# Decoder of two layers: the order of steps in the context product, and of the first expert block's preparation in layer 1

## The chip, the cores and the metric

The kernel runs on one core of one Trainium2 chip. The metric is the device time of one execution in microseconds (us), as the median of the runs shown. A core has five engines, each with its own queue that it works through in program order: PE (TensorE, matrix products), DVE (VectorE), ACT (ScalarE), POOL (GpSimd) and SP (SyncE, which here only issues DMA transfers). The engines wait for one another through semaphores, and an instruction that waits holds up everything behind it on its engine.

## What is computed

A decoder of two layers over x of 4 batches x 512 tokens x 256 features. Cut to what the change touches:

```python
x = x + attn0(layernorm(x))                       # causal, 16 heads
# context product, the same context for all three factors
x1 = einsum('eth,efh->etf', layernorm(x), ctx)    # 512 x 256 by 512 x 256, for each of 4 batches
x2 = x1
x = x + einsum('etf,efh->eth', gelu(x1) * x2, ctx)
x = x + moe0(layernorm(x))                        # 8 experts of width 512, two per token, and a shared one
x = x + attn1(layernorm(x)); x = x + cross(layernorm(x), ctx)
# layer 1's experts: 8 of width 1024, the best two per token, weighted
for e in range(8):
    h = silu(x @ w1[e].T) * (x @ w3[e].T)
    out = out + wte[:, e:e+1] * (h @ w2[e].T)
x = x + out
```

## The kernel before

The stages stand one behind the other, each in a block of its own: attention, `geglu` (the context product), `moe` for layer 0, two attentions, `moe` for layer 1.

**The context product** (`geglu`, L948) goes batch by batch. Its parts are written once for each engine, and `run` gives all engines the same order of steps: LN (normalise a batch: DVE statistics, two small POOL operations, four DVE operations that write `xn`), T (eight PE transposes into `t_ps`, two DVE copies to `xnT`), G (eight PE products into the four banks of `g_ps`; for each bank ACT forms `gelu`, then DVE multiplies it into `h`), Y (two halves of eight PE products into `y_ps`, each added to x by DVE), IN (SP loads the context). The profile lists each product of G and Y twice, so that G has sixteen rows there and each Y sixteen. Batch 0's LN and T come first. Then a hardware loop runs over batches 0 to 2 with the body in `body(b, nxt)`, and the same body without a next batch follows for batch 3. In the body, LN and T of the next batch stand between steps of this one.

**The experts of layer 1** (`moe`, with `moe_schedule` as the order that all engines share). Tokens are sorted into blocks of rows, each with one expert: blocks 0, 1 and 2 are large (256 rows), block 3 is small, and so on. A block n is worked in chunks f = 0 to 3 of the hidden width. All float32 weights and rows are split in two parts, hi (ACT copies) and lo (DVE subtracts), and a product is made in three passes. The steps and what they stand for:

- SPOT and LIST: which token stands in which row (one-hot products on PE). LISTS and GATHER: the lists are read and POOL gathers the first rows.
- UNMASKED, EXP, SHARES: the routing weights (DVE, ACT for the exponential, DVE). WEIGHTS: POOL multiplies them into `held`, six operations. LIST with part 2: 64 PE products that bring the weights into row order, which read `held` and the one-hot tiles. These tiles lie in the memory of `raw2`, so that block 0's w2 is loaded (WEIGHED, on SP) only when they have been read; WEIGHED on DVE reads the result.
- T n: rows of block n transposed on PE, split by ACT and DVE (`rows_hi`, `rows_lo`); POOL gathers the rows of block n + 2.
- C 0 f: split of w1 and w3 of block 0, chunk f (ACT two operations, DVE two); SP then loads the same chunk for block 1. W n f: the same for block n, and the load for n + 1.
- CV: split of block 0's w2 (four operations on ACT, four on DVE); SP then loads block 1's. V n f: the same for later blocks.
- G n f: 24 PE products into one of two slots of `g_ps`; ACT forms silu, DVE multiplies (`late`, the step's `h_made`). The slot is free for the chunk after next once DVE has done so. H n f: the split of that product (`h_hi` on ACT, `h_lo` on DVE).
- Y n t: 24 PE products with w2 for half t of block n. Y 0 0 waits for the whole of CV, and for WEIGHED.
- IDLE: products without use that keep PE at work.

`chunk(n, f)` writes G, then the W that `weights_beside(n, f)` names, then H (in the last chunk of a block H comes ahead of W), then what `between` has at the number n * 4 + f. For block 0 the W beside chunk f is W 1 f, and CV stands in `between` at chunk 1.

Semaphores carry all of this. A step changes place on all engines at once, since one list sets the order for all.

Of the kernel before, what the change touches and what calls it, by code (L numbers as in the profile page):

```python
# [29 lines left out]
B, T, D = 4, 512, 256  # L30
# [914 lines left out]
def geglu(nc, tag, x, const, w):  # L945


    with ExitStack() as ctx:  # L948
# [40 lines left out]
        def run(eng, do):  # L989
            def step(kind, *at):  # L990
                if kind in do:
                    do[kind](*at)

            step("LN", 0)
            step("T", 0)

            def body(b, nxt):
                step("IN", b)
                step("G", b)
                if nxt is not None:  # L1000
# [180 lines left out]
def moe_schedule(shared, nf):  # L1181
# [4 lines left out]
    def small(n):  # L1186
        return n >= nshared and halves(n - nshared) == 1
# [32 lines left out]
    else:  # L1220
# [24 lines left out]
        yield "C", 0, 0  # L1245
        yield "UNMASKED", 1, 0
        yield "EXP", 1, 0
        yield "C", 0, 1

        yield "IDLE", 24, 0  # L1250
        yield "T", 0, 0
        yield "IDLE", 5, 0
        yield "SHARES", 0, 0
        yield "WEIGHTS", 0, 0
        for f in range(2, nf):
            yield "C", 0, f
        between = {1: [("LIST", c, 2) for c in range(NSPOT)] + [("WEIGHED", 0, 0), ("CV", 0, 0)]}

    def prepared(n, *chunks):
        if n < nblocks:  # L1260
            for f in chunks:
                yield "W", n, f


    def weights_beside(n, f):
        if nf > 2 and n and small(n - 1):
            return (n + 1, f - 1) if f else (n, nf - 1)
        if nf > 2 and n > 1 and small(n - 2) and f == 0:
# [990 lines left out]
```

## Time and profile before

| | us |
|---|---|
| median of 3 runs | 1727.65 (1726.07 to 1731.89) |
| time of the profiled execution | 1731.58 |
| span of its profile | 1729.8 |
| PE busy | 1489.5 (86%) |
| DVE busy | 1177.9 (68%) |
| ACT busy | 900.3 (52%) |
| POOL busy | 553.0 (32%) |
| context product, from the first IDLE product to the last product | 300.3 to 376.3 |
| layer 1's experts, last PE product of the first token list to the first product of Y 0 0 | 1339.5 to 1380.8 |

Times in the profile count from the span's start. PE, DVE, ACT and POOL are busy times; the stages have different limits, so that the shares say little and the order of time in a stage says much. "Idle before" in a row is the time for which the engine stood still ahead of it, and the name behind the arrow is what ended that.

### The profile page before, as it was taken

How to read it: one execution, taken by the hardware profiler on the slowest of the kernel's cores; microseconds unless marked ns; L12 is line 12 of the kernel's file. 1: busy time of each engine (PE TensorE's matmuls, PEld its weight loads, DVE VectorE, ACT ScalarE, POOL GpSimd, SP SyncE). 2: the span in 40 equal slices, each digit the busy share in tenths (PEclk: the TensorE clock that was granted, in tenths of full speed). 3: DMA queues.
4: the chain of work that ended last, by engine and by line, in shares of the span. 5: the costliest groups of instructions: out<-in, count | busy, mean ns of one | idle time of the engine just before them, and what ended most of it. 6: DMA issues, size and time to landing. Idle time of an engine off the chain costs nothing. (4 is left out here: it accounts for less than half of the span.)

```text
span 1729.8 us, 30585 instructions
## 1 busy us (share of the span) xinstructions
PE 1489.5 (86%) x10462; PEld 1015.4 (59%) x10462; DVE 1177.9 (68%) x2008; ACT 900.3 (52%) x1704; POOL 553.0 (32%) x765
## 2 busy tenths in 40 slices
PE   7989987889899996798888878878864799999996
PEld 3445453559899996333333333223223699999996
DVE  5565552454778885667677636776767778888884
ACT  2444453123256664146555465676761466767763
POOL 6344440010236554725343340110011323333321
PEclk8999998998999999789999989888887899999999
DMA  6223220220258884422222131222203468777782
GB/s 166 43 44 57 43 52 7 65 88 32 98 178 248 249 255 114 129 57 52 41 43 63 35 68 39 62 50 52 45 14 133 163 205 244 241 237 239 247 232 65
DMA packets 104266, 194.36 MB, mean 112 GB/s; under 512 B 30417, under 2 KB 55762, under 8 KB 101170
## 3 DMA queue, kind: packets, MB, share of 16 engines
q1 hardware_dynamic: 75186, 157.78, 29.3%
q0 software_dynamic: 28416, 34.25, 11.2%
q8 instruction: 84, 1.38, 0.3%
q14 instruction: 68, 0.56, 0.1%
q10 hardware_dynamic: 512, 0.40, 0.1%
HBM read 135.63 MB, written 18.61 MB: 89 GB/s over the span
## 5 line engine op out<-in xcount | busy, mean ns | idle before, releaser
L719 ACT ACTIVATE l1a_sb_probs<-l1a_s_ps,l1a_sb_kmax 128x512 f32<-128x512 f32 x256 | 172.5, 708 | 74.2 <-issue 59.8
L617 DVE TENSOR_REDUCE l1a_sb_mx<-l1a_s_ps 128x2 f32<-128x1024 f32 x128 | 154.2, 1219 | 62.7 <-PE l1a_s_ps L805 62.7
L651 DVE TENSOR_REDUCE l1a_sb_kmax<-l1a_s_ps 128x2 f32<-128x1024 f32 x128 | 154.1, 1216 | 45.2 <-PE l1a_s_ps L846 44.2
L725 ACT ACTIVATE l1a_sb_probs<-l1a_s_ps 128x1024 f32<-128x1024 f32 x128 | 128.0, 1022 | 89.4 <-PE l1a_s_ps L846 88.8
L617 DVE TENSOR_REDUCE l0a_sb_mx<-l0a_s_ps 128x2 f32<-128x256 f32 (+3 forms) x128 | 103.5, 821 | 77.4 <-PE l0a_s_ps L818 76.0
L1927 PE MATMUL l1m_g_ps<-l1m_sb_rows_hi,l1m_sb_hi 128*128 128x256 f32 x512 | 147.2, 287 | 6.8 <-DVE l1m_sb_late L1825 6.4
L846 PE MATMUL l1a_s_ps<-l1a_sb_qst,l1a_sb_kst 49*128 49x512 f32 (+1 forms) x512 | 130.4, 516 | 24.1 <-ACT l1a_sb_probs L719 22.5
L846 PEld LDWEIGHTS l1a_s_ps<-l1a_sb_qst,l1a_sb_kst 49*128 49x128 f32 (+1 forms) x512 | 50.1, 195 | 168.8 <-issue 86.5
L1927 PE MATMUL l1m_g_ps<-l1m_sb_rows_lo,l1m_sb_hi 128*128 128x256 f32 x512 | 145.7, 285 | 0.0
L1927 PE MATMUL l1m_g_ps<-l1m_sb_rows_hi,l1m_sb_lo 128*128 128x256 f32 x512 | 145.7, 284 | 0.0
L1799 DVE TENSOR_TENSOR l1m_sb_lo<-l1m_sb_raw,l1m_sb_hi 128x512 fp32r<-128x512 f32 x184 | 121.8, 704 | 19.6 <-ACT l1m_sb_hi L1710 18.7
L1660 POOL DMA_INDIRECT out_x<-l1m_sb_late,l1m_sb_add_to x39 | 65.7, 1684 | 176.0 <-DVE l1m_sb_late L1847 171.1
L725 ACT ACTIVATE l0a_sb_probs<-l0a_s_ps 128x1024 f32<-128x1024 f32 (+3 forms) x128 | 87.3, 698 | 64.3 <-PE l0a_s_ps L818 64.1
L1927 PE MATMUL l0m_g_ps<-l0m_sb_rows_hi,l0m_sb_hi 128*128 128x256 f32 x384 | 113.7, 296 | 7.1 <-DVE l0m_sb_rows_lo L1793 6.6
L507 POOL DMA_DIRECT2D l1a_sb_kst<-l1a_sb_hi x156 | 76.8, 496 | 133.1 <-PE l1a_s_ps L846 128.9
L1927 PE MATMUL l0m_g_ps<-l0m_sb_rows_hi,l0m_sb_lo 128*128 128x256 f32 x384 | 111.7, 291 | 0.0
L1927 PE MATMUL l0m_g_ps<-l0m_sb_rows_lo,l0m_sb_hi 128*128 128x256 f32 x384 | 111.6, 291 | 0.0
L1710 ACT ACTIVATE l1m_sb_hi<-l1m_sb_raw 128x512 fp32r<-128x512 f32 x184 | 104.8, 620 | 0.0
L1927 PEld LDWEIGHTS l1m_g_ps<-l1m_sb_rows_hi,l1m_sb_hi 128*128 128x128 f32 x512 | 99.2, 194 | 7.4 <-issue 6.6
L1927 PEld LDWEIGHTS l1m_g_ps<-l1m_sb_rows_hi,l1m_sb_lo 128*128 128x128 f32 x512 | 99.1, 194 | 0.0
L1927 PEld LDWEIGHTS l1m_g_ps<-l1m_sb_rows_lo,l1m_sb_hi 128*128 128x128 f32 x512 | 99.0, 193 | 0.0
L507 POOL DMA_DIRECT2D l0a_sb_kst<-l0a_sb_hi x124 | 61.2, 498 | 98.5 <-PE l0a_s_ps L818 59.4
(410 smaller groups left out, 4018.3 us busy)
## 6 DMA issues: line engine op xcount, KB each, us to landing
l1m_sb_raw<-in_l1m_w SPq DMA_DIRECT2D x92, 512.0 KB
l0m_sb_raw<-in_l0m_w SPq DMA_DIRECT2D x72, 512.0 KB
l1m_sb_raw<-in_l1m_w SPq DMA_DIRECT2D x23, 1024.0 KB
l1a_sb_qst<-l1a_sb_hi SPq DMA_DIRECT2D x256, 32.0 KB, 2.0
l1a_sb_kst<-l1a_sb_hi POOLq DMA_DIRECT2D x156, 32.0 KB, 2.0
l0a_sb_qst<-l0a_sb_hi SPq DMA_DIRECT2D x128, 32.0 KB, 2.0
l1a_sb_qst<-l1a_sb_lo SPq DMA_DIRECT2D x128, 32.0 KB, 2.0
l0a_sb_kst<-l0a_sb_hi POOLq DMA_DIRECT2D x124, 32.0 KB, 2.0
```

What stands on the lines that cost most here:

```text
L507: pool.dma_start(in_stack(kst, p, e, n), in_part(source, i, p, e)).then_inc(kstacked[p], 16)
L617: dve.tensor_reduce(mx[:, g, qt, 2 * p:2 * p + 2], buffer("A", b, g, j)[:, :, 0:last], AX.X, ALU.max).then_inc(a_max.sem, 1)
L651: dve.tensor_reduce(kmax[:, n % 4, :], buffer("S", b, g, j)[:, :, :], AX.X, ALU.max, negate=True).then_inc(kmax_done.sem, 1)
L719: ins = act.activation(probs[:, n % 8, e, :], at[:, e, :], ACT.Exp, bias=kmax[:, n % 4, e:e + 1], accum_out=zsum[:, n % 4, e:e + 1])
L725: act.activation(probs[:, n % 8, :, c0:T], at[:, :, c0:T], ACT.Exp, scale=SCALE).then_inc(exp_done.sem, 1)
L846: ins = pe.matmul(at[:, e, c0:T], kst[rows, p, kt * P:(kt + 1) * P], qst[rows, p, c0:T], start=True, stop=not causal)
L1660: pool.indirect_dma_start(total, bass.IndirectOffsetOnAxis(ap=at, axis=0), y[:, e % 2, t, :], None, compute_op=ALU.add).then_inc(stored[e ...
L1710: ins = act.activation(two_chunks(hi, s % 2, f), raw13[:, s % n13, f, n, :, :], ACT.Copy)
L1799: ins = dve.tensor_tensor(two_chunks(lo, s % 2, f), raw13[:, s % n13, f, n, :, :], two_chunks(hi, s % 2, f).bitcast(F32), ALU.subtract)
L1927: ins = pe.matmul(at, s, m, start=n == 0, stop=n == len(passes) - 1)
```

## The change

In the context product's body, LN of the next batch moves ahead of this batch's G, and T of the next batch moves from between the two Y to ahead of both. In `moe_schedule`, for the layer whose blocks have four chunks (layer 1): SHARES and WEIGHTS move from behind T 0 to ahead of the idle products and T 0; C 0 1 moves from ahead of the idle products to behind T 0; C 0 2 and C 0 3 move from ahead of G 0 0 to behind G 0 0 and G 0 1; the W of block 1 move one chunk back, with W 1 3 directly ahead of G 1 0; CV moves from behind chunk 1 of block 0 to behind chunk 0 of block 1. Layer 0's experts keep their order.

```diff
             def body(b, nxt):
                 step("IN", b)
+
+                if nxt is not None:
+                    step("LN", nxt)
                 step("G", b)
                 if nxt is not None:
-                    step("LN", nxt)
+                    step("T", nxt)
                 step("Y", b, 0)
-                if nxt is not None:
-                    step("T", nxt)
                 step("Y", b, 1)
...
         yield "UNMASKED", 1, 0
         yield "EXP", 1, 0
-        yield "C", 0, 1
+        yield "SHARES", 0, 0
+        yield "WEIGHTS", 0, 0
 
         yield "IDLE", 24, 0
         yield "T", 0, 0
         yield "IDLE", 5, 0
-        yield "SHARES", 0, 0
-        yield "WEIGHTS", 0, 0
-        for f in range(2, nf):
-            yield "C", 0, f
-        between = {1: [("LIST", c, 2) for c in range(NSPOT)] + [("WEIGHED", 0, 0), ("CV", 0, 0)]}
+        yield "C", 0, 1
+
+        between = {1: [("LIST", c, 2) for c in range(NSPOT)] + [("WEIGHED", 0, 0)], nf: [("CV", 0, 0)]}
...
     def weights_beside(n, f):
-        if nf > 2 and n and small(n - 1):
+        if nf > 2 and n == 0:
+
+            return (1, f - 1) if f else (1,)
+        if nf > 2 and small(n - 1):
             return (n + 1, f - 1) if f else (n, nf - 1)
...
+        if nf > 2 and n == 1 and f == 0:
+            yield from prepared(1, nf - 1)
         yield "G", n, f
+        if nf > 2 and n == 0 and f < 2:
+            yield "C", 0, f + 2
```

In the context product's loop, PE's queue from the last bank of G to the loop's end, before: `l0g_y_ps` is Y, `l0g_t_ps` the transposes T; the rows without names are register work.

```order
L1085 MATMUL l0g_g_ps<-l0g_sb_xnT,l0g_sb_ctxT 128x512 x2
L58 ISA x2
L1096 MATMUL l0g_y_ps<-l0g_sb_ctxN,l0g_sb_h 128x256 x8
L58 ISA
L58 REGISTER_ALU
L1075 MATMUL l0g_t_ps<-const_ident,l0g_sb_xn 128x128 x8
L58 REGISTER_ALU
L1096 MATMUL l0g_y_ps<-l0g_sb_ctxN,l0g_sb_h 128x256 x8
```

And after:

```order
L1086 MATMUL l0g_g_ps<-l0g_sb_xnT,l0g_sb_ctxT 128x512 x2
L58 ISA
L58 REGISTER_ALU
L1076 MATMUL l0g_t_ps<-const_ident,l0g_sb_xn 128x128 x8
L58 ISA x2
L1097 MATMUL l0g_y_ps<-l0g_sb_ctxN,l0g_sb_h 128x256 x8
L58 REGISTER_ALU
L1097 MATMUL l0g_y_ps<-l0g_sb_ctxN,l0g_sb_h 128x256 x8
```

The transposes now stand directly behind G, and the two Y are back to back.

DVE's queue in the same loop, before, from the end of LN (`l0g_sb_xn`) to the end of the body: add of Y's first half to x, the two copies of T, add of the second half. The four products of the gates (`l0g_sb_h`) and LN's statistics stand ahead of this.

```order
L1132 TENSOR_SCALAR l0g_sb_xn<-x_sb,l0g_sb_mv,l0g_sb_rstd 128x256 x4
L58 REGISTER_ALU
L1040 ISA
L1040 TENSOR_TENSOR x_sb<-l0g_y_ps,x_sb 128x512
L58 REGISTER_ALU
L1047 COPY l0g_sb_xnT<-l0g_t_ps 128x512 x2
L1040 ISA
L1040 TENSOR_TENSOR x_sb<-l0g_y_ps,x_sb 128x512
```

And after:

```order
L1133 TENSOR_SCALAR l0g_sb_xn<-x_sb,l0g_sb_mv,l0g_sb_rstd 128x256 x4
L58 ISA
L1036 TENSOR_TENSOR l0g_sb_h<-l0g_g_ps,l0g_sb_gelu 128x512 x4
L58 REGISTER_ALU
L1048 COPY l0g_sb_xnT<-l0g_t_ps 128x512 x2
L58 REGISTER_ALU
L1041 ISA
L1041 TENSOR_TENSOR x_sb<-l0g_y_ps,x_sb 128x512
L1041 ISA
L1041 TENSOR_TENSOR x_sb<-l0g_y_ps,x_sb 128x512
```

The four gate products now stand behind the whole of LN, and the copies stand directly behind them.

DVE's queue in layer 1's experts, before, from WEIGHED (`row_holds`, `row_weight`) on. L1805 is CV, L1825 the gate product of a chunk, L1799 the lo part of a w1 and w3 chunk (two each), L1831 the lo part of the gate product.

```order
L2149 COPY l1m_sb_row_holds<-l1m_y_ps 128x2x69
L2151 TENSOR_TENSOR l1m_sb_row_weight<-l1m_sb_row_holds 128x46
L2152 TENSOR_TENSOR l1m_sb_row_weight<-l1m_sb_row_weight,l1m_sb_row_holds 128x46
L1805 TENSOR_TENSOR l1m_sb_lo<-l1m_sb_raw,l1m_sb_hi 128x512 x4
L1825 TENSOR_TENSOR l1m_sb_late<-l1m_g_ps,l1m_sb_late 128x512
L1799 TENSOR_TENSOR l1m_sb_lo<-l1m_sb_raw,l1m_sb_hi 128x2x256 x2
L1831 TENSOR_TENSOR l1m_sb_h_lo<-l1m_sb_late,l1m_sb_h_hi 128x512
```

And after, the stretch of the same queue that ends with CV (now L1812), from the gate product of chunk 3 of block 0 on; in this version the gate product is L1832, the w1 and w3 parts L1806, the lo part of the gate product L1838:

```order
L1832 TENSOR_TENSOR l1m_sb_late<-l1m_g_ps,l1m_sb_late 128x512
L1838 TENSOR_TENSOR l1m_sb_h_lo<-l1m_sb_late,l1m_sb_h_hi 128x512
L1806 TENSOR_TENSOR l1m_sb_lo<-l1m_sb_raw,l1m_sb_hi 128x2x256 x4
L1832 TENSOR_TENSOR l1m_sb_late<-l1m_g_ps,l1m_sb_late 128x512
L1806 TENSOR_TENSOR l1m_sb_lo<-l1m_sb_raw,l1m_sb_hi 128x2x256 x2
L1838 TENSOR_TENSOR l1m_sb_h_lo<-l1m_sb_late,l1m_sb_h_hi 128x512
L1812 TENSOR_TENSOR l1m_sb_lo<-l1m_sb_raw,l1m_sb_hi 128x512 x4
```

CV stood directly behind WEIGHED, ahead of the gates of chunks 2 and 3 of block 0; it now stands behind these two, behind W 1 1 to W 1 3 and W 2 0, and behind the gate of chunk 0 of block 1.

## Rows read from the trace of the kernel before

**Rows 1.** The page, part 1: PE's busy time, share of the span and instructions.
```profile
PE 1489.5 (86%) x10462; PEld 1015.4 (59%) x10462; DVE 1177.9 (68%) x2008; ACT 900.3 (52%) x1704; POOL 553.0 (32%) x765
```

**Rows 2.** Timeline, PE, context product (start us, length us, instructions, idle before).
```profile
325.08 7.03 PE L1085 MATMUL l0g_g_ps<-l0g_sb_xnT,l0g_sb_ctxT 128*128 128x512 f32 x16
333.68 3.71 PE L1096 MATMUL l0g_y_ps<-l0g_sb_ctxN,l0g_sb_h 128*128 128x256 f32 x16 [1.57 <-DVE l0g_sb_h L1035]
338.49 1.09 PE L1075 MATMUL l0g_t_ps<-const_ident,l0g_sb_xn 128*128 128x128 f32 x8 [1.10 <-DVE l0g_sb_xn L1132]
339.42 3.62 PE L1096 MATMUL l0g_y_ps<-l0g_sb_ctxN,l0g_sb_h 128*128 128x256 f32 x16
342.87 7.03 PE L1085 MATMUL l0g_g_ps<-l0g_sb_xnT,l0g_sb_ctxT 128*128 128x512 f32 x16
```

**Rows 3.** Timeline, DVE, context product.
```profile
305.76 1.29 DVE L1047 COPY l0g_sb_xnT<-l0g_t_ps 128x512 f32<-128x512 f32 x2 [0.75 <-PE l0g_t_ps L1075]
...
325.41 0.69 DVE L1040 TENSOR_TENSOR x_sb<-l0g_y_ps,x_sb 128x512 f32 x1 [2.74 <-PE l0g_y_ps L1096]
329.09 1.29 DVE L1035 TENSOR_TENSOR l0g_sb_h<-l0g_g_ps,l0g_sb_gelu 128x512 f32<-128x512 f32 x2 [2.99 <-ACT l0g_sb_gelu L1061]
...
332.85 0.69 DVE L1035 TENSOR_TENSOR l0g_sb_h<-l0g_g_ps,l0g_sb_gelu 128x512 f32<-128x512 f32 x1 [1.02 <-ACT l0g_sb_gelu L1061]
333.46 1.40 DVE L1119 BATCH_NORM_STATS2 l0g_sb_stats<-x_sb 128x6 f32 x4
...
336.98 1.38 DVE L1132 TENSOR_SCALAR l0g_sb_xn<-x_sb,l0g_sb_mv,l0g_sb_rstd 128x256 f32 x4 [1.51 <-POOL l0g_sb_rstd L1111]
```

**Rows 4.** Timeline, PE, layer 1's experts, blocks 0 and 1.
```profile
1359.98 2.02 PE L1899 MATMUL l1m_y_ps<-l1m_sb_held,l1m_sb_raw 128*128 128x69 bf16 x32 [3.48 <-issue]
1361.82 1.62 PE L1899 MATMUL l1m_y_ps<-l1m_sb_held,l1m_sb_late 128*128 128x69 bf16 x32
...
1375.70 0.55 PE L1927 MATMUL l1m_g_ps<-l1m_sb_rows_hi,l1m_sb_hi 128*128 128x256 f32 x1 [6.44 <-DVE l1m_sb_late L1825]
...
1379.68 0.36 PE L1927 MATMUL l1m_g_ps<-l1m_sb_rows_hi,l1m_sb_hi 128*128 128x256 f32 x1
...
1380.83 0.36 PE L1927 MATMUL l1m_y_ps<-l1m_sb_hi,l1m_sb_h_hi 128*128 128x256 f32 x1
...
1383.78 0.28 PE L1927 MATMUL l1m_g_ps<-l1m_sb_rows_hi,l1m_sb_hi 128*128 128x256 f32 x1
```

**Rows 5.** Timeline, ACT, layer 1's experts.
```profile
1346.13 0.31 ACT L1693 ACTIVATE l1m_sb_l<-l1m_sb_l 128x128 f32<-128x128 f32 x1 [4.31 <-DVEq L2042]
...
1371.72 2.19 ACT L1717 ACTIVATE l1m_sb_hi<-l1m_sb_raw 128x512 fp32r<-128x512 f32 x4 [8.82 <-DMA l1m_sb_raw<-in_l1m_w]
```

**Rows 6.** Timeline, SP, the issue of the first two loads of w2.
```profile
1364.72 11.30 SPq L1531 DMA_DIRECT2D l1m_sb_raw<-in_l1m_w  x2
```

**Rows 7.** Timeline, POOL, the six products of WEIGHTS.
```profile
1353.04 6.85 POOL L1677 TENSOR_TENSOR l1m_sb_held<-l1m_sb_own,l1m_sb_share 128x368 bf16<-128x368 bf16 x6 [1.92 <-DVEq L2090]
```

**Rows 8.** Timeline, DVE, layer 1's experts.
```profile
1349.31 0.69 DVE L1793 TENSOR_TENSOR l1m_sb_rows_lo<-l1m_t_ps,l1m_sb_rows_hi 128x512 fp32r<-128x512 f32 x1 [0.51 <-issue]
...
1353.04 4.97 DVE L1799 TENSOR_TENSOR l1m_sb_lo<-l1m_sb_raw,l1m_sb_hi 128x512 fp32r<-128x512 f32 x4
1357.94 0.68 DVE L1825 TENSOR_TENSOR l1m_sb_late<-l1m_g_ps,l1m_sb_late 128x512 f32<-128x512 f32 x1
...
1372.45 2.50 DVE L1805 TENSOR_TENSOR l1m_sb_lo<-l1m_sb_raw,l1m_sb_hi 128x512 fp32r<-128x512 f32 x4 [7.61 <-ACT l1m_sb_hi L1717]
...
1375.47 1.28 DVE L1799 TENSOR_TENSOR l1m_sb_lo<-l1m_sb_raw,l1m_sb_hi 128x512 fp32r<-128x512 f32 x2
...
1387.49 0.69 DVE L1825 TENSOR_TENSOR l1m_sb_late<-l1m_g_ps,l1m_sb_late 128x512 f32<-128x512 f32 x1 [2.66 <-ACT l1m_sb_late L1736]
```

**Rows 9.** Windows: busy of PE, PEld, DVE, ACT, POOL (instructions), granted clock, DMA share, GB/s.
```profile
1375.00:1380.00 5.00, 4.30 (x21) 4.33 (x22) 3.96 (x7) 3.21 (x6) 0.00 (x0) 0.52 0.58 211
```

**Rows 10.** Waits of PE from 1380 us to the end (total, times, longest).
```profile
PE l1m_y_ps L1927 <- issue: 3.2, 2, 2.8
```

## The prediction

> **What bounds the kernel now.** I read the page first: PE is busy for 1489.5 us of 1729.8, the largest share [rows 1], so what counts is where PE stands still or works slowly, and who ends that. Then PE's timeline in the two stages that the change touches, and beside each of its gaps the timeline of the engine named there.
>
> *Context product.* One turn of the loop takes 342.87 - 325.08 = 17.79 us of PE [rows 2]. In it the reader is to see two gaps: 1.57 us ahead of the first Y, until DVE has multiplied the last gate, and 1.10 us ahead of the transposes T, until DVE has normalised the next batch. From the first Y to the next G it is 342.87 - 333.68 = 9.19 us. DVE starts LN only when the last gate is done (at 333.46), and LN runs to 336.98 + 1.38 = 338.36, 4.90 us [rows 3].
>
> *Layer 1's experts.* PE waits twice between the first rows and Y 0 0 [rows 4]. 3.48 us, until 1359.98, ahead of the products that order the weights: POOL works on WEIGHTS until 1353.04 + 6.85 = 1359.89 [rows 7]. And 6.44 us, until 1375.70, ahead of G 1 0: it needs the slot of G 0 2, whose gate stands on ACT and DVE behind CV; ACT stood 8.82 us in front of CV for w2's transfer, until 1371.72 [rows 5]. Behind that wait PE is also slow: 19 products from 1375.70 to 1379.68, 0.21 us each, and the granted clock in this window is 0.52, the lower level of 1.2 GHz; from 1379.68 on it is 0.12 us (24 products from 1380.83 to 1383.78) [rows 4, 9]. After 1380 PE waits for 3.2 us in all up to the end [rows 10]: PE bounds the rest, and what is won before Y 0 0 reaches the end of the kernel.
>
> **The context product after the change.** T moves into the gap ahead of the first Y. T keeps PE for 339.42 - 338.49 = 0.93 us, the gap is 1.57 us, and xn must be there by then. The two Y then stand back to back at 342.87 - 339.42 = 3.45 us each, 6.90 together; the old 9.19 us shrink by 2.29 us in each of the three turns, 6.9 us in all.
>
> What it costs is that the gates now queue behind LN on DVE. In a turn that begins with G at time 0, DVE ends the last add at 325.41 + 0.69 - 325.08 = 1.02 us [rows 2, 3]; LN then takes 4.90 us (its 1.51 us wait for POOL included) and ends at 5.92. T needs it at 7.03, when G ends: free by 1.1 us. The gates started at 4.01 before; now the first three of them run from 5.92, 0.61 us each (333.46 - 332.85), to 7.75, and the fourth waits for its gelu until 7.77 (332.85 - 325.08) as before. So LN is hidden in the time in which DVE waited for gelu, with nothing to spare: whatever DVE takes to go round the loop moves the first Y one to one, in two turns (the first turn has 1 us to spare: there LN starts when the copies of batch 0 end, 305.76 + 1.29 = 307.05 [rows 3], and with them G). No row shows that time alone. Its bounds: nothing (PE goes round without a gap, 339.42 + 3.45 = 342.87), and 2.99 us, the idle time in which it lies before [rows 3]. I take 0.2 us, near PE's, since DVE too only steps a counter and branches: 0.4 us for two turns. The copies of T follow the fourth gate, and DVE has nothing else before the adds; POOL's two operations keep their distance to LN; SP's step IN keeps its place. Gain 6.9 - 0.4 = **6.5 us**, with bounds 6.9 and 6.9 - 2 x 2.95 = 1.0.
>
> **Layer 1's experts after the change.** I walk through the queues.
>
> *SHARES first.* The exponential ends at 1346.44 [rows 5]. SHARES fills the time from the end of rows_lo, 1350.00, to 1353.04: 3.0 us [rows 8]. Now it runs from 1346.5 to 1349.5, where DVE waited and did C 0 1; T 0's rows_lo follows at 1349.5 instead of 1349.31, and G 0 0 starts 0.2 us later. POOL starts WEIGHTS at 1349.7 and, if it is as slow as before (6.85 us), ends at 1356.5. PE ends G 0 1 at 1359.98 - 3.48 + 0.2 = 1356.7: the first wait is gone. C 0 1 to C 0 3 are hidden: POOL's products make a DVE lo part cost 4.97 / 4 = 1.24 us instead of 1.28 / 2 = 0.64 [rows 8], so C 0 1 is done at 1350.2 + 2.5 = 1352.7, before G 0 1 wants it at 1353.6; C 0 2 and C 0 3 at 1357.7 and 1360.2 at the latest, before 1359.6 and 1362.5.
>
> Beside POOL's products, the DVE row with a source in PSUM keeps its 0.68 us (1357.94) [rows 8], so I charge rows_lo nothing. The Trainium skill ("SBUF — State Buffer", section "SBUF: two separate sides") has DVE with two inputs in SBUF contend with GpSimd for a port pair held as an exclusive lock; rows_lo has one input there and escapes by it as well. Were it slowed like the others, G 0 0 would start 0.6 us later and the gain be 0.6 us less.
>
> *To the end of G 0 3.* The weights' products take 2 x 1.45 = 2.9 us at their second half's pace to 3.3 us as before (1363.27 - 1359.98, where the first 32 took 1.84) [rows 4], so G 0 2 starts at 1359.6 to 1360.0. G 0 2 and G 0 3 take 2.95 us each: G 0 3 ends at 1365.5 to 1365.9. G 1 0 has its slot (gate of G 0 2 at about 1364.4) and W 1 0, runs at once and ends at 1368.4 to 1368.8, T 2 0.5 us later.
>
> *Then a new wait.* Y 0 0 needs CV, and CV now stands last in a long queue on DVE. From the gate of G 0 3 on DVE has the list that the order shows: gate, h_lo, four lo parts, gate, two lo parts, h_lo, CV's four: 14 operations, 13 x 0.61 + 0.68 = 8.6 us, and 1.1 us of handovers from ACT (0.7 ahead of the h_lo, 0.35 ahead of W 1 2), 9.7 us. The gate comes 0.8 us behind its chunk's end on PE (1387.49 against 1383.78 + 2.9) [rows 4, 8]. Y 0 0 can start at 1365.7 + 0.8 + 9.7 = 1376.2, after a wait of about 7 us. Before it started at 1380.83: 4.6 us earlier. W2's load is hidden: SP issues it behind the load for W 1 0 at about 1362.7, 2.0 us earlier than before (1364.72 [rows 6]); before it took 7.0 us to 1371.72, so it lands at 1369.7, and ACT wants it at 1372.1. The price of this cover, should it fail, is one to one.
>
> *And the clock.* The new wait is as long as the old one of 6.44 us, behind which 19 products ran at the lower level. The same 19 products of Y 0 0 would lose 3.98 - 19 x 0.12 = 1.7 us. The next chunk, G 1 1, starts 4.6 - 1.7 = **2.9 us** earlier than at 1383.78. Bounds: 4.6 (no slow products) and 1.0 (each of DVE's six lo parts of w1 and w3 stretched by 0.3 us). From the skill's page "TensorE: Matmul & The Clock Gate", section "What's actually happening": the same kernel shows 6, 11 or 14 slow products depending on the phase. By 6 instead of 19 the loss would be 0.6 us and this gain 4.0; the trace here has 19, and I stay with them.
>
> Behind CV, w2 of block 1 is asked for at about 1377.3 instead of 1376.0; V 1 0 waits for Y 0 1, not before 1386.5, and 7 us lie between: free.
>
> **The sum.** 6.5 + 2.9 = 9.4 us. The profiled execution took 1731.58 us, 3.9 above the median; it would become 1722.2, and the median 1727.65 - 9.4 = **1718.2 us**.
>
> **The rivals.**
> - *CV's wait costs all of it.* DVE's chain to CV ends 4.6 - 1.7 = 2.9 us or more later than I have it (POOL's gathers beside the lo parts, or w2 landing after 1375), and only the context product gains: 1727.65 - 6.5 = 1721.2. For it: the chain is long and I have each operation at its best pace. Against: POOL's products are over by 1356.5, and behind them two lo parts take 1.28 us [rows 8].
> - *Both waits go and none comes.* Then the experts win 3.48 + 6.44 + 1.7 = 11.6 us: 1709.5. Against: the order puts CV behind the 14 operations, and nothing else holds Y 0 0.
> - *DVE's way round the loop is dear.* With 1.6 us in place of 0.2 the context product gains 6.9 - 3.1 = 3.8 us: 1727.65 - 3.8 - 2.9 = 1721.0.
> - *Slower.* w2 is late at CV. It is issued behind two loads of 0.5 MB for block 1 and 2. Each microsecond that it lands after 1372.1 moves Y 0 0. To eat both gains and 0.3% more it would have to land 6.5 + 2.9 + 5.2 = 14.6 us late, at 1386.7, 24 us after its issue against 7.0 before: 1732.8 or more.
> - *The change doesn't do what it says.* The order shows every move on every engine; no weight on this.
>
> **Chances.** Mine 0.66; CV costs all 0.14; loop dear 0.09; both waits gone 0.07; slower 0.02; nothing won, by an effect that I don't see, 0.02. My own case spans 1714.7 (bounds 6.9 and 4.6, and 1.5 us of scatter) to 1721. The range 1712.5 to 1723.0 takes in the two cases at 1721, and leaves out the case at 1709.5 and the worst. A measurement of this kernel tells about 0.3% (5.2 us) from no change; faster by that is below 1722.5: 0.88. Within it: 0.09. Slower: 0.03.
>
> **What would show it.** Right: turns of about 15.7 us in the context product, T directly behind G, PE's only gap about 0.6 us ahead of the first Y; no wait ahead of the weights' products; G 1 0 directly behind G 0 3; a wait of about 7 us ahead of Y 0 0, released by DVE's lo part of w2, with slow products behind it. Wrong: a turn above 16.5 us (the loop); Y 0 0 released by a DMA behind ACT (w2); no wait at Y 0 0 (the chain); or PE waiting more after Y 0 0 than 3.2 us.

## The result and the profile after

In rounds taken in turn with the kernel before, the changed kernel takes 1721.11 us against 1732.03 us (medians of 20 runs each): the ratio is 0.9946, with a 95% interval of 0.9932 to 0.9959. That is 9.3 us less (7.1 to 11.8), where 9.4 were forecast. The two medians by themselves differ by 10.9 us, inside that interval. One of the 12 runs of e1 below took 1796 us at a granted clock of 0.81 and is left out of its ratio. In these rounds the kernel before stood 4.4 us higher than in the three runs that the prediction started from; so the time comes out at 1721.1 where 1718.2 was named.

The profiled execution of the changed kernel took 1731.05 us, the slowest of its 20. Its span, 1729.2 us, stands beside 1729.8 for the kernel before: the two traces seem to show no gain at all. So I read the gain stage by stage, from places that both kernels have in common. The first is the row of idle products ahead of a stage (TensorE, line 98). First the kernel before, then the changed kernel (timeline of PE: start us, length us, instructions, idle before):

```profile
300.30 4.88 PE L98 MATMUL l0g_g_ps<-const_ones_b 128*128 128x512 bf16 x12 [2.32 <-PEq L225]
...
377.36 2.96 PE L98 MATMUL l0m_g_ps<-const_ones_b 128*128 128x512 bf16 x13 [1.05 <-PEq L948]
...
1339.28 5.96 PE L98 MATMUL l1m_g_ps<-const_ones_b 128*128 128x512 bf16 x20
```

```profile
304.69 1.87 PE L98 MATMUL l0g_g_ps<-const_ones_b 128*128 128x512 bf16 x4 [2.32 <-PEq L225]
...
375.18 4.48 PE L98 MATMUL l0m_g_ps<-const_ones_b 128*128 128x512 bf16 x20 [1.05 <-PEq L948]
...
1341.26 4.01 PE L98 MATMUL l1m_g_ps<-const_ones_b 128*128 128x512 bf16 x9
```

| stretch | before | changed | difference |
|---|---|---|---|
| start to the context product | 300.30 | 304.69 | +4.39 |
| context product | 377.36 - 300.30 = 77.06 | 375.18 - 304.69 = 70.49 | **-6.57** |
| to the first idle product of layer 1's experts | 961.92 | 966.08 | +4.16 |
| from there to G 1 1 | 1383.78 - 1339.28 = 44.50 | 1381.69 - 1341.26 = 40.43 | **-4.07** |

In this pair of traces 10.6 us are won in the two places of the change and 8.6 us are lost in two stretches that it doesn't touch. In those TensorE does the same work for longer, at a lower granted clock. In the windows (columns as in [rows 9]) the instructions before the context product are the same to one; first before, then changed:

```profile
0.00:300.50 300.50, 260.13 (x2465) 141.06 (x2466) 159.52 (x270) 125.67 (x201) 118.72 (x221) 0.95 0.27 59
377.50:1339.30 961.80, 799.84 (x4896) 482.76 (x4895) 678.26 (x1145) 514.81 (x1026) 311.95 (x452) 0.91 0.36 95
```

```profile
0.00:304.50 304.50, 264.31 (x2464) 143.73 (x2464) 159.33 (x269) 125.86 (x201) 118.31 (x221) 0.93 0.27 58
375.00:1341.00 966.00, 804.41 (x4889) 484.96 (x4890) 678.60 (x1144) 515.17 (x1026) 313.50 (x452) 0.90 0.36 95
```

2464 matrix products keep PE for 4.2 us more at a clock of 0.93 instead of 0.95. The experiments below show the same stretch between 297.5 and 304.7 us long, whatever the kernel: it belongs to the execution, not to the change. Behind G 1 1 another 1.5 us are lost, all at the kernel's end. There PE stands still for 2.85 us in both kernels. Its last 48 products (the last block's Y) then take 5.71 us from the first start to the last in the kernel before and 7.19 us in the changed one, where 17 of them are 0.21 us apart (granted clock 0.50 from 1711.60 to 1715.00). DVE's last product waits for them, 7.61 us instead of 6.12, and POOL's last writes of the output wait for DVE. This isn't the change's doing either: e3 and e4 below, with the experts' order of before, show 7.20 and 7.19 us. From the first idle product of the experts to the end the pair of traces so shows 390.50 - 387.95 = 2.55 us of the 4.07. PE's waits behind Y 0 0 are 3.2 us in all, as before [rows 10].

**The context product after** (timeline of PE, then of DVE; they answer to [rows 2] and [rows 3]):

```profile
327.27 7.03 PE L1086 MATMUL l0g_g_ps<-l0g_sb_xnT,l0g_sb_ctxT 128*128 128x512 f32 x16
334.14 1.04 PE L1076 MATMUL l0g_t_ps<-const_ident,l0g_sb_xn 128*128 128x128 f32 x8
335.87 7.17 PE L1097 MATMUL l0g_y_ps<-l0g_sb_ctxN,l0g_sb_h 128*128 128x256 f32 x32 [0.70 <-DVE l0g_sb_h L1036]
342.88 1.45 PE L1086 MATMUL l0g_g_ps<-l0g_sb_xnT,l0g_sb_ctxT 128*128 128x512 f32 x3
```

```profile
327.60 0.69 DVE L1041 TENSOR_TENSOR x_sb<-l0g_y_ps,x_sb 128x512 f32 x1 [2.76 <-PE l0g_y_ps L1097]
328.28 1.41 DVE L1120 BATCH_NORM_STATS2 l0g_sb_stats<-x_sb 128x6 f32 x4
...
331.83 1.38 DVE L1133 TENSOR_SCALAR l0g_sb_xn<-x_sb,l0g_sb_mv,l0g_sb_rstd 128x256 f32 x4 [1.50 <-POOL l0g_sb_rstd L1112]
333.12 2.61 DVE L1036 TENSOR_TENSOR l0g_sb_h<-l0g_g_ps,l0g_sb_gelu 128x512 f32<-128x512 f32 x4
335.66 1.28 DVE L1048 COPY l0g_sb_xnT<-l0g_t_ps 128x512 f32<-128x512 f32 x2
```

A turn is 342.88 - 327.27 = 15.61 us. T stands directly behind G, both Y follow in one row of 32, and PE's only gap is 0.70 us ahead of them. On DVE the end of the last add (328.29) and LN's first row (328.28) touch, though the step round the loop lies between them.

**Layer 1's experts after** (timeline of PE; the rows of [rows 4]). To compare with the kernel before, take 1.98 us off, by which the first idle product is later here:

```profile
1358.73 1.21 PE L1906 MATMUL l1m_y_ps<-l1m_sb_held,l1m_sb_raw 128*128 128x69 bf16 x32
1359.78 1.20 PE L1906 MATMUL l1m_y_ps<-l1m_sb_held,l1m_sb_late 128*128 128x69 bf16 x32
1360.81 0.36 PE L1934 MATMUL l1m_g_ps<-l1m_sb_rows_hi,l1m_sb_hi 128*128 128x256 f32 x1
...
1369.53 0.60 PE L1927 MATMUL l1m_t_ps<-const_ident,l1m_sb_rows 128*128 128x128 f32 x4
...
1377.31 0.58 PE L1934 MATMUL l1m_y_ps<-l1m_sb_hi,l1m_sb_h_hi 128*128 128x256 f32 x1 [7.18 <-DVE l1m_sb_lo L1812]
...
1381.69 0.28 PE L1934 MATMUL l1m_g_ps<-l1m_sb_rows_hi,l1m_sb_hi 128*128 128x256 f32 x1
```

No wait is left ahead of the list's products, and they take 2.08 us (3.29 before). G 1 0 has no wait. A wait of 7.18 us stands ahead of Y 0 0, and DVE's lo part of w2 (CV) ends it. Behind it the first 14 products of Y 0 0 are 0.21 us apart and the rest 0.12: the chunk takes 4.38 us instead of 2.95. The list's products of the kernel before ran for the most part at the lower clock, 0.50 in this window of its trace (columns as in [rows 9]); in the changed kernel the clock was 1.00 throughout:

```profile
1360.00:1361.00 1.00, 1.00 (x19) 1.00 (x19) 1.00 (x3) 1.00 (x3) 0.97 (x1) 0.50 0.83 332
```

The wait's cause in the timelines of DVE and SP (they answer to [rows 8] and [rows 6]):

```profile
1367.48 0.69 DVE L1832 TENSOR_TENSOR l1m_sb_late<-l1m_g_ps,l1m_sb_late 128x512 f32<-128x512 f32 x1
...
1369.91 2.54 DVE L1806 TENSOR_TENSOR l1m_sb_lo<-l1m_sb_raw,l1m_sb_hi 128x512 fp32r<-128x512 f32 x4 [0.35 <-ACT l1m_sb_hi L1717]
...
1374.77 2.48 DVE L1812 TENSOR_TENSOR l1m_sb_lo<-l1m_sb_raw,l1m_sb_hi 128x512 fp32r<-128x512 f32 x4
```

```profile
1364.38 0.33 SPq L1538 DMA_DIRECT2D l1m_sb_raw<-in_l1m_w  x1
```

From the gate of G 0 3 (1367.48) to CV's end (1377.25) it is 9.8 us, without a gap longer than 0.7: DVE's queue is the wait. ACT's part of CV starts at 1373.62 behind other work of ACT, not behind a DMA: the load of w2 is hidden, by 1.5 us (7.7 us from its issue at 1364.38 to its landing). POOL's six products of WEIGHTS take 5.50 us here (6.85 in [rows 7]), since only part of them meets work of DVE. In their time rows_lo keeps its 0.69 us (at 1351.70), and the two lo parts behind it take 1.94 us instead of 1.29. By the Trainium skill ("SBUF — State Buffer", section "SBUF: two separate sides") a DVE operation with two inputs in SBUF contends with a GpSimd operation that reads SBUF for a shared pair of ports; the trace agrees, with 1.94 us for the two lo parts (both inputs in SBUF) and an unchanged 0.69 us for rows_lo (one input in SBUF).

### The profile page after: what moved, and what is told of

The parts are those of the page before. It is cut to its first block and busy times, and to the rows that moved or that the text cites. A ratio compares the mean times of both kernels' runs of the same rounds, so it can differ in the third digit from the quotient of the medians.

```text
span 1729.2 us, 30572 instructions
## 1 busy us (share of the span) xinstructions
PE 1498.6 (87%) x10462; PEld 1021.1 (59%) x10462; DVE 1175.8 (68%) x2008; ACT 900.7 (52%) x1704; POOL 551.7 (32%) x765
## 5 line engine op out<-in xcount | busy, mean ns | idle before, releaser
L1806 DVE TENSOR_TENSOR l1m_sb_lo<-l1m_sb_raw,l1m_sb_hi 128x512 fp32r<-128x512 f32 x184 | 119.3, 691 | 18.4 <-ACT l1m_sb_hi L1717 17.6
L1934 PE MATMUL l1m_y_ps<-l1m_sb_hi,l1m_sb_h_hi 128*128 128x256 f32 x312 | 90.9, 291 | 10.4 <-DVE l1m_sb_lo L1812 7.2
```

Of the source, the lines that this page charges most:

```text
L1806: ins = dve.tensor_tensor(two_chunks(lo, s % 2, f), raw13[:, s % n13, f, n, :, :], two_chunks(hi, s % 2, f).bitcast(F32), ALU.subtract)
L1934: ins = pe.matmul(at, s, m, start=n == 0, stop=n == len(passes) - 1)
```

## The experiments

Where times are compared inside a stage, zero is the first of the 24 idle products ahead of T 0 ("+" below). **G 1 1** is +44.50 us before and +40.43 after the change. A later mark, the first product of the G chunk behind block 1's early ones (1434.46 before, 1432.37 changed), is called **mark B**: +95.18 and +91.11. In the changed kernel the gain is the same at both, 4.07 us. These are single executions. Where the experts' order is that of before, G 1 1 is at +44.50, +44.14 (e1), +44.00 (e3) and +44.54 (e4); where it is the changed one, at +40.43, +40.41 (e2) and +41.14 (a1). So the experts' gain at this mark is 2.9 to 4.1 us, and a shift of half a microsecond in one trace says nothing.

### One half of the change at a time

**e1: the context product alone** (the first piece of the change's diff; the second stage as before).

> Only the context product's part of the change; the experts keep the order of before. My theory: the two parts add, and this one gives 6.5 us (6.6 in the trace of the changed kernel, from the first idle product of the stage to the first of the next: 77.06 us become 70.49), so the time is 0.9962 of before. Rival A: the gain in the stage is given back further on, because the stages behind it start elsewhere in the clock's course; then the stage is 6.6 us shorter and the time is within 2 us of before. Rival B: the clock phase makes the gain, the order does not; then the stage is longer than 72 us here.

Measured: 1724.46 us against 1730.39, ratio 0.9963 (0.9945 to 0.9981), 6.4 us less (3.3 to 9.5): rivals A and B are both out, by the time and by the stage. The stage takes 367.95 - 297.47 = 70.48 us, 6.58 less than before, and the turns are the changed kernel's. In the experts the list's wait of 3.48 us is there, and G 1 0 still waits for the gate:

```profile
1360.57 0.56 PE L1928 MATMUL l1m_g_ps<-l1m_sb_rows_hi,l1m_sb_hi 128*128 128x256 f32 x1 [5.97 <-DVE l1m_sb_late L1826]
```

**e2: the experts alone** (the other pieces of the diff).

> Only the experts' part of the change; the context product keeps the order of before. My theory: 4.1 us (the changed kernel's trace has G 1 1 at 40.43 us behind the first of the 24 idle products, before it was 44.50), 0.9976 of before; a wait of about 7.2 us at Y 0 0, released by DVE's lo part of w2. Rival: I forecast 2.9 us from the same chain with 19 slow products and slow list products; then G 1 1 stands 41.6 us behind the first idle product and the changed kernel was lucky by 1.2.

Measured: 1727.0 against 1730.39, ratio 0.998 (0.9965 to 0.9995), 3.5 us less (0.9 to 6.1). The context product takes 375.59 - 298.55 = 77.04 us, as before. Y 0 0 starts at +36.05, G 1 1 at +40.41, mark B at +91.09: each within 0.02 us of the changed kernel. The rival's +41.6 doesn't show here; a1 below, at +41.14, comes half way to it.

```profile
1373.51 0.58 PE L1933 MATMUL l1m_y_ps<-l1m_sb_hi,l1m_sb_h_hi 128*128 128x256 f32 x1 [7.19 <-DVE l1m_sb_lo L1811]
```

What follows: the halves don't touch each other. Ratios multiply to 0.9943 against 0.9946 for the whole, and the stages add up: 6.58 + 4.09 = 10.7 us against 10.6.

### Inside the context product

**e3: LN ahead of G, T left between the two Y.**

```diff
 step("IN", b)
-step("G", b)
 if nxt is not None:
     step("LN", nxt)
+step("G", b)
 step("Y", b, 0)
 if nxt is not None:
     step("T", nxt)
 step("Y", b, 1)
```

> Of the context product only LN ahead of G; T stays between the two Y. My theory: the wait of 1.10 us ahead of T goes, T itself (0.93 us) stays on PE between the Y, so a turn of the loop is 17.79 - 1.10 = 16.7 us against 15.6 with both, and the stage 3.4 us shorter than before (73.7 us). Rival (LN first is what gives everything, T's place is of no matter): turns of 15.6 us.

**e4: T behind G, LN left behind G's gates.**

```diff
 step("G", b)
 if nxt is not None:
     step("LN", nxt)
+    step("T", nxt)
 step("Y", b, 0)
-if nxt is not None:
-    step("T", nxt)
 step("Y", b, 1)
```

> Of the context product only T ahead of both Y; LN stays behind the gates on DVE. My theory: T waits for LN, which starts when the last gate is multiplied (8.38 us behind G's start) and takes 4.90 us; T then 0.93, two Y 6.90, so a turn is 8.38 + 4.90 + 0.13 + 0.93 + 0.17 + 6.90 = 21.4 us, and the stage 77.1 + 3 x 3.6 = 87.9 us, 10.8 us slower than before. Rival (LN is hidden anyway by the time that PE needs for the gates): turns of 15.6 to 17.8 us. PE idles some 6 us a turn in one gap, so that the lower clock may add 1 us a turn.

Measured, e3: 1723.14 us in one run; the stage 373.46 - 300.36 = 73.10 us, a turn 340.30 - 323.82 = 16.48. PE's timeline has T without a wait and keeps the 1.57 us ahead of the first Y:

```profile
332.42 3.71 PE L1097 MATMUL l0g_y_ps<-l0g_sb_ctxN,l0g_sb_h 128*128 128x256 f32 x16 [1.57 <-DVE l0g_sb_h L1036]
335.97 1.04 PE L1076 MATMUL l0g_t_ps<-const_ident,l0g_sb_xn 128*128 128x128 f32 x8
...
340.30 4.88 PE L1086 MATMUL l0g_g_ps<-l0g_sb_xnT,l0g_sb_ctxT 128*128 128x512 f32 x11
```

Measured, e4: 1750.43 us in one run; the stage 396.95 - 301.54 = 95.41 us, a turn 332.62 - 308.81 = 23.81, 6.0 more than before. The timeline of PE and the windows over T's wait and behind it:

```profile
322.33 1.96 PE L1074 MATMUL l0g_t_ps<-const_ident,l0g_sb_xn 128*128 128x128 f32 x8 [6.39 <-DVE l0g_sb_xn L1131]
324.08 8.70 PE L1095 MATMUL l0g_y_ps<-l0g_sb_ctxN,l0g_sb_h 128*128 128x256 f32 x32
332.62 7.03 PE L1084 MATMUL l0g_g_ps<-l0g_sb_xnT,l0g_sb_ctxT 128*128 128x512 f32 x16
```

```profile
315.70:322.30 6.60, 0.24 (x1) 0.00 (x0) 3.76 (x14) 0.60 (x1) 1.21 (x2) 0.87 0.26 81
322.30:332.60 10.30, 10.27 (x40) 9.02 (x41) 2.08 (x3) 0.00 (x0) 0.00 (x0) 0.75 0.00 0
```

The reader is to see two costs. PE waits 6.39 us for xn, in the place of the old gaps of 1.57 and 1.10: 3.7 us a turn. And T and both Y take 332.62 - 322.33 = 10.29 us, where at the full clock they take 0.93 + 6.90 = 7.8 [rows 2]: 2.4 us more a turn, at a granted clock of 0.75 in that window. I had expected the first cost, and of the second 1 us a turn at most and none in the sum, so 18.3 us were lost and not 10.8.

What follows: LN first wins 3.96 us by itself. T's move by itself loses 18.3, and on top of LN first it wins another 2.6. Only the order LN, G, T, Y, Y has both.

### Inside the experts

**e5: SHARES and WEIGHTS ahead of the idle products, C 0 1 behind T 0 with C 0 2 and C 0 3, all else as before.**

```diff
-yield "C", 0, 1
+yield "SHARES", 0, 0
+yield "WEIGHTS", 0, 0
 yield "IDLE", 24, 0
 yield "T", 0, 0
 yield "IDLE", 5, 0
-yield "SHARES", 0, 0
-yield "WEIGHTS", 0, 0
-for f in range(2, nf):
+for f in range(1, nf):
     yield "C", 0, f
```

> The kernel before with one edit in layer 1's first block: SHARES and WEIGHTS stand ahead of the 24 idle products and of T 0; CV stays between C 0 1 and G 0 0's successors as before, the context product as before. My theory (the two waits are separate, and this edit takes away the first alone): TensorE's idle 3.48 us ahead of the list's second product goes, and the list's products take 2.1 to 3.3 us; the 6.44 us ahead of Y 0 0 are a DMA's (w2 of block 0, which SP issues behind other loads and on which ACT waited 8.82 us), so part of what is won returns there: Y 0 0 starts 1 to 4 us earlier than before's +41.55 us after the first idle product, G 1 0's start likewise. Rival (the waits are one budget: the DMA alone sets Y 0 0): Y 0 0 stays at +41.5 us within 0.3 and the wait ahead of it grows to about 9.9 us.

**e6: CV behind G 0 3 instead of behind the list, all else as before.**

```diff
-between = {1: [("LIST", c, 2) for c in range(NSPOT)] + [("WEIGHED", 0, 0), ("CV", 0, 0)]}
+between = {1: [("LIST", c, 2) for c in range(NSPOT)] + [("WEIGHED", 0, 0)], nf: [("CV", 0, 0)]}
```

> The kernel before with one edit in layer 1's first block: CV (the split of w2 of block 0) stands behind block 0's last gate product instead of ahead of the second gate. My theory: the list's wait of 3.48 us stays; DVE and ACT no longer stand at CV's wait for the DMA while block 0's gates end, and Y 0 0 starts when gate 3's chain and CV's four splits are through: 1.0 us earlier than before's +41.55 us (0.5 to 2.5). Together with the weights-first edit it should make the 5.50 us that Y 0 0 moved in the changed kernel: gains of the two single edits that add to about 5.5 us say they are independent; a sum far below says that each is worth something only with the other. Rival (CV behind the gates costs all its 2.5 us on the path): Y 0 0 at +42 to +44 us.

Measured, e5: the list's wait is gone, and G 1 0 waits for longer (PE). ACT stands in front of the DMA as before, and SP shows why (ACT, then SP):

```profile
1370.73 0.55 PE L1926 MATMUL l1m_g_ps<-l1m_sb_rows_hi,l1m_sb_hi 128*128 128x256 f32 x1 [9.83 <-DVE l1m_sb_late L1824]
```

```profile
1366.75 2.19 ACT L1716 ACTIVATE l1m_sb_hi<-l1m_sb_raw 128x512 fp32r<-128x512 f32 x4 [9.48 <-DMA l1m_sb_raw<-in_l1m_w]
```

```profile
1359.08 11.97 SPq L1530 DMA_DIRECT2D l1m_sb_raw<-in_l1m_w  x2
```

SP issues w2's load at +23.93, behind the loads of w1 and w3 as before and only 1.5 us earlier (+25.44 [rows 6]); w2 is there at 1366.75, +31.60, where it was +32.44 [rows 5]. G 1 0 starts 0.84 us earlier than before, G 1 1 0.45, mark B 0.43. This is the rival's case, close to the letter (Y 0 0 at +41.10, 0.45 earlier where the rival allows 0.3): 3.48 us of wait were taken away and at most 0.45 were won, since the DMA ends the next wait. G 1 1, at +44.06, lies among the four executions with the order of before (+44.00 to +44.54), so even the 0.45 may be nothing.

Measured, e6: Y 0 0 starts at +38.22, 3.3 us earlier than before, where I expected 1.0. But Y 0 0 was the wrong mark: G 1 0 stood behind the wait before, and now stands ahead of it. At G 1 1, behind both, it is +43.50: 1.0 us. At mark B it is 0.64, because the half clock reaches into G 1 1. Nor is the 1.0 us shown to be CV's. The list's products, ahead of CV's new place, take 2.06 us here and 3.29 in the kernel before, and G 0 2 starts 1.07 us earlier. From G 0 2 to G 1 1 it takes 20.59 us here, 20.51 before, and 20.06 to 21.38 in e1, e3 and e4. The list's products differ between executions of one order: in e4, which has the experts' order of before, they run at the full clock too, behind a wait of 2.48 us:

```profile
1376.30 1.19 PE L1898 MATMUL l1m_y_ps<-l1m_sb_held,l1m_sb_raw 128*128 128x69 bf16 x32 [2.48 <-issue]
```

And e6 itself (PE):

```profile
1357.41 1.20 PE L1899 MATMUL l1m_y_ps<-l1m_sb_held,l1m_sb_raw 128*128 128x69 bf16 x32 [2.35 <-issue]
...
1374.78 0.58 PE L1927 MATMUL l1m_y_ps<-l1m_sb_hi,l1m_sb_h_hi 128*128 128x256 f32 x1 [5.99 <-DVE l1m_sb_lo L1805]
```

The list's products still wait for POOL, so that G 0 2 starts at +22.91, where the changed kernel has +19.55, and everything behind it is later.

What follows: at G 1 1, against the four executions with the order of before, e5 alone wins nothing that is clear of their scatter and e6 alone 0.5 to 1.0 us; the whole change wins 2.9 to 4.1. The prediction treated the moves as a walk through one queue and was right to. No run has these two edits together without the change's other moves (C 0 2 and C 0 3 behind the gates, the W of block 1 one chunk back). Leg by leg, as an estimate from the traces: G 0 2 at +19.76 as in e5 and 15.3 us from there to Y 0 0 as in e6 give +35.1, against +36.05 in the changed kernel; w2, which is there at +31.60 in e5, would come about 0.3 us late for ACT. So the two edits may well be enough for the gain, and that the other moves help is not shown.

### What the 7.18 us are

**e7: CV directly behind H 0 3 in the changed kernel; the weight splits of blocks 1 and 2 put off behind it.**

```diff
-between = {1: [...("WEIGHED", 0, 0)], nf: [("CV", 0, 0)]}
+between = {1: [...("WEIGHED", 0, 0)], nf - 1: [("CV", 0, 0)]}
+put_off = {(0, 0): (), (0, 1): (), (0, 2): ((1, 0),), (0, 3): (), (1, 0): ((1, 1), (1, 2)),
+           (1, 1): ((1, 3), (2, 0)), (1, 2): ((2, 1), (2, 2)), (1, 3): ((2, 3),)}
...
-        if nf > 2 and n == 1 and f == 0:
-            yield from prepared(1, nf - 1)
...
-        yield from prepared(*weights_beside(n, f))
+        if nf > 2 and (n, f) in put_off:
+            for m, g in put_off[n, f]:
+                yield from prepared(m, g)
+        else:
+            yield from prepared(*weights_beside(n, f))
```

> The changed kernel with CV moved directly behind H 0 3's first operations, ahead of the weight splits of blocks 1 and 2, which are put off by one or two gates. My theory (the 7.18 us ahead of Y 0 0 are DVE's queue: gate 3's chain with other splits mixed in, then CV): the wait falls to 2 to 3 us, few or no products at the half clock follow, and G 1 1 starts 4 to 6 us earlier than the changed kernel's +40.43 us; the time falls to 0.991 to 0.993 of before's. Rival (the wait is handed on): the splits of blocks 1 and 2 that were put off end late, and TensorE waits at G 1 1 or G 1 2 for them for what Y 0 0 won; then Y 0 0 is early, and block 1's last Y stands where the changed kernel has it, time 0.9945 as in the changed kernel.

**e8: the changed kernel with 30 idle products in the wait.**

```diff
-if new_set(n) or n == 0:
+if new_set(n) or n == 0 and shared:
     w2_done.wait(pe, s, NF - 1)
...
+if n == 0 and not shared:
+    keep_warm(pe, y_ps[:, 0, :, :].rearrange("p t d -> p (t d)"), const, 30)
+    w2_done.wait(pe, s, NF - 1)
```

> The changed kernel with 30 idle products of 128x128 into Y 0 0's own tile (each overwritten by Y 0 0's first product) in the 7.18 us wait ahead of Y 0 0. Nothing of the result changes. My theory (the products of Y 0 0 are slow since the engine stood idle for 7.18 us): the idle products run in the wait, Y 0 0 starts where it did (+36.05 us) and its products take 0.12 us each from the first one on, and G 1 1 starts 1.4 us earlier than +40.43 us. Rival (slow for another reason, as operands late one by one): 15 products at 0.21 us as before, and +40.4 us.

Measured, e7: 1719.64 against 1732.22 us, ratio 0.9933 (0.9908 to 0.9958). Timeline of PE:

```profile
1352.11 0.26 PE L1907 MATMUL l1m_y_ps<-l1m_sb_held,l1m_sb_late 128*128 128x69 bf16 x3 [0.42 <-issue]
1352.85 0.42 PE L1907 MATMUL l1m_y_ps<-l1m_sb_held,l1m_sb_late 128*128 128x69 bf16 x8 [0.48 <-issue]
...
1364.30 0.39 PE L1935 MATMUL l1m_y_ps<-l1m_sb_hi,l1m_sb_h_hi 128*128 128x256 f32 x1 [1.44 <-DVE l1m_sb_lo L1813]
```

Y 0 0 starts at +32.05 behind a wait of 1.44 us, no product is slow, and G 1 1 is at +35.03, 5.4 us earlier than in the changed kernel. So DVE's queue was the wait, as the earlier CV took 5.7 us of it away. But 2.05 us are given back: a new wait of 1.67 us stands ahead of Y 1 0, for the h_lo of G 1 3, and mark B is at +87.76, 3.35 us earlier than in the changed kernel. Theory and rival each got a part.

Measured, e8: 1718.10 us in one run. The trace shows the 30 idle products as 128x512; they keep PE at work for 6.64 us of the wait. PE's timeline at Y 0 0 and the windows over the wait and over Y 0 0:

```profile
1366.33 0.39 PE L1934 MATMUL l1m_y_ps<-l1m_sb_hi,l1m_sb_h_hi 128*128 128x256 f32 x1 [0.72 <-DVE l1m_sb_lo L1812]
1366.55 0.28 PE L1934 MATMUL l1m_y_ps<-l1m_sb_hi,l1m_sb_h_lo 128*128 128x256 f32 x1
```

```profile
1358.90:1366.30 7.40, 6.71 (x33) 2.90 (x30) 7.38 (x13) 5.74 (x11) 1.98 (x2) 1.00 0.63 213
1366.30:1369.30 3.00, 2.97 (x24) 2.98 (x25) 0.57 (x1) 0.00 (x0) 0.00 (x0) 1.00 0.66 209
```

The granted clock stays at 1.00, the products of Y 0 0 are 0.12 us apart from the second on, and the chunk takes 2.98 us instead of 4.38: the 1.40 us that I expected. G 1 1 is only 0.16 us earlier (+40.27), since the list's products took 3.43 us in this execution and put G 0 2 1.23 us later; from G 0 2 to Y 0 0 it is 16.51 us, against 16.50 in the changed kernel. That the slow products come of the engine's standing still is shown (0 of them here and in e7, 14 to 27 behind every wait of 5.5 us or more); that the kernel as a whole gains by the idle products is not.

### One more split put off, and the changed kernel again

**e10: as e7, with one split of block 2 put off by one more gate.**

```diff
-(1, 2): ((2, 1), (2, 2)), (1, 3): ((2, 3),)}
+(1, 2): ((2, 1),), (1, 3): ((2, 2), (2, 3))}
```

> The kernel with CV directly behind H 0 3 (e7), with one weight split of block 2 (W 2 2: two tiles, 1.25 us of DVE) moved from behind gate (1, 2) to behind gate (1, 3). My theory (the 1.67 us at Y 1 0 are the 2.49 us of splits of block 2 that DVE takes between gate 1 2 and gate 1 3): that wait falls to about 0.4 us, and block 1's end stands 1.2 us earlier than e7's, 4.6 us earlier than the changed kernel's (the time 0.992 to 0.993 of before's). Rival (the wait is handed on again): the split that was moved is late for G 2 2, and the landmark behind block 1 stands where e7 has it, +87.8 us.

**a1: the changed kernel once more, without an edit.**

> The changed kernel itself once more, on the chip and in the rounds of e10. By the stages, G 1 1 stands at +40.4 us and the landmark behind block 1 at +91.1 us after the first idle product, and the ratio to the kernel before is 0.9946 within 0.0015, 3 to 5 us above e10's in the same rounds. It also shows whether the list's second product (2.08 us from its first row to the gate behind it in the trace of the changed kernel, 3.4 us in e7's and e8's) differs between executions of one kernel: if it comes out at 3.4 us here, it isn't the kernel that makes the difference.

Measured in the same rounds, against 1732.68 us for the kernel before: e10 1719.99, ratio 0.9926 (0.9897 to 0.9955); a1 1721.41, ratio 0.9929 (0.9908 to 0.9949). The two can't be told apart by time, where I expected 3 to 5 us between them; a1's ratio is also 0.0017 below the 0.9946 of the result, a little more than I allowed, and the two intervals overlap. The stages of e10: from G 1 1 to Y 1 0 it takes 15.39 us where e7 took 16.60, and the wait at Y 1 0 is 0.47: the split was the cause, and nothing came in its place. But mark B is at +89.09, behind e7's +87.76. The loss lies ahead of the edit, where both kernels have the same order (timelines of PE and ACT):

```profile
1365.56 0.38 PE L1935 MATMUL l1m_y_ps<-l1m_sb_hi,l1m_sb_h_hi 128*128 128x256 f32 x1 [3.00 <-DVE l1m_sb_lo L1813]
```

```profile
1362.34 2.19 ACT L1725 ACTIVATE l1m_sb_hi<-l1m_sb_raw 128x512 fp32r<-128x512 f32 x4 [1.52 <-DMA l1m_sb_raw<-in_l1m_w]
```

SP issued w2's load at 1355.17, it took 7.2 us, and ACT stood 1.52 us in front of it; in e7 ACT didn't wait. CV as early as this puts w2's load back on the path, and whether it costs something differs from one execution to the next. Behind the 3.00 us PE ran 17 products at the half clock, 1.5 us.

Of the two later kernels both are faster than the kernel before beyond doubt; that one of them beats the changed kernel is suggested by the marks (-3.35 and -2.0 us at mark B, each in a single execution) and not shown by the times.

a1's stages are the changed kernel's: context product 372.74 - 302.23 = 70.51 us, Y 0 0 at +36.04 behind 7.18 us, the list's products 2.08 us. Only the slow products differ: 22 and not 14, 5.10 us and not 4.38, so G 1 1 is at +41.14 and mark B at +91.84.

## Why the prediction was right, step by step

- **Turns of the context product**: 15.7 forecast, 15.61 measured. T in the gap, both Y back to back, LN hidden in DVE's wait for gelu: all as worked out.
- **DVE's way round the loop**: 0.2 us taken, with bounds of 0 and 2.99. It costs nothing that the trace can show (328.29 to 328.28), and the first Y starts 8.60 us behind G as before; the rival "loop dear" falls. But the two Y back to back take 342.88 - 335.87 = 7.01 us and not 6.90, 0.3 us over three turns. That 6.57 us came out for 6.5 is so in part luck: a cost that was taken and didn't come, and one that came and wasn't taken, nearly cancel. (Of the bounds, 6.9 - 2 x 2.99 is 0.9, not 1.0.) e3 and e4 show that both moves are needed.
- **SHARES first**: G 0 0 0.2 us later forecast; it starts at +11.18, where the kernel before has +10.78: 0.4. WEIGHTS end in time, and the first wait is gone, as forecast.
- **The list's products** are the term that was mis-sized: 2.9 to 3.3 us forecast, 2.08 measured. I took their time from rows that ran for the most part at the lower clock [rows 4]; in the changed kernel they ran at the full clock throughout. That isn't the removed wait's doing alone: with the experts' order of before they took 3.29, 3.45 (e1) and 3.34 us (e3), but 2.06 in e4 and e6, behind waits of 2.48 and 2.35 us. G 0 2 starts at +19.55 and was forecast at 1359.6 at the earliest, which is +20.3.
- **The chain to CV**: 9.7 us forecast, 9.8 measured; the wait ahead of Y 0 0 about 7 us, measured 7.18; w2's load hidden, as forecast. Y 0 0 came 5.5 us earlier, forecast 4.6; the 0.9 us between them are the list's products.
- **The slow products**: 19 taken, for 1.7 us; 14 measured, for 1.4, and 22 in a1, for 2.15. By the Trainium skill ("TensorE: Matmul & The Clock Gate", section "What's actually happening") the number of slow products at a kernel's start differs between executions of one kernel; behind this wait the traces show the same, with 14 and 22. The page's smallest number, 6, shows nowhere behind a wait of this length. With 5.5 - 1.4 the experts' gain at G 1 1 is 4.07 us in this pair instead of 2.9, inside its bounds of 1.0 and 4.6, and 2.9 to 4.1 over all the traces.
- **From there to the end**: forecast was that what is won before Y 0 0 reaches the end. PE's waits say so (3.2 us in both kernels), the clock doesn't: 1.5 of the 4.07 us are gone at the end in this pair of traces.
- **The sum**: 9.4 us forecast; the stages show 10.6, and the paired runs 9.3 (7.1 to 11.8), a1's 12.3 (8.8 to 15.9). The mechanism is as forecast in every term; that the number is met within 0.1 us is luck, since the list's products alone are 0.8 to 1.2 us off and the intervals are over 4 us wide. The rival "CV costs all" is out by e2: the experts alone are at 0.998 (0.9965 to 0.9995), and G 1 1 is at least 2.9 us earlier. The time of e1 wouldn't settle it, since its interval overlaps the changed kernel's. "Both waits gone" is out by the 7.18 us.

## What to carry to other kernels

Price an edit by walking each queue through the new order to the next place that all engines have in common, and take as the mark a place behind everything that was reordered. Waits that stand one behind the other don't add: of 3.48 us taken away alone at most 0.45 were won, and the whole change won 2.9 to 4.1 at the same mark. Before you price work by its rows, look at the granted clock they ran at. Before you believe a shift of a mark, look where other executions of the same order have it.

## What the runs showed of the hardware

- **Executions of one kernel differ by more than this change wins.** The stretch from the start to the context product, the same in all kernels here, took 297.47 us (e1) to 304.69 (changed), at a granted clock of 0.97 to 0.93; the stretch between the two stages 955.63 (e3) to 968.07 us (a1). The changed kernel's 20 runs lie between 1716.6 and 1731.1 us. A single span says nothing on a change of 10 us. Marks inside the touched stage are better, but not always: up to Y 0 0 they repeated within 0.02 us in the changed order (after, e2, a1: +36.05, +36.05, +36.04), while G 1 1 in the order of before moved by 0.54 us between four executions, with the place of the stretches at the lower clock.
- **The clock behind a wait.** Behind 1.44 us (e7) no product ran at half rate; behind 3.00 us (e10) four ran at full rate and then 17 at half; behind 5.56 to 9.83 us those at half rate came at once, 14 to 27 of them (14 in the changed kernel and e2, 18 in e4, 19 before, 22 in e1 and a1, 23 in e3 and e5, 27 in e6). With idle products in the wait (e8) there were none. Shorter waits went either way: behind the 2.85 us at the kernel's end of the last 48 products 13 to 27 ran at half rate in eight executions and none in four (before, e1, e5, e7), and that costs 1.2 to 2.6 us.
- **Left open**: the list's second product showed two gaps of 0.42 and 0.48 us in e7, and like ones in e8, released by nothing that the trace names; e10, with e7's order up to there, has none, and neither have the changed kernel, e2 and a1, whose order up to there is that of e8.
